# Spreading reciprocal softmax sums over partitions: by TensorE or by small DMAs through DRAM

## What is computed

```python
# second stage: t is (4, 1024, 64)
q, k, v = x @ Wq.T, x @ Wk.T, x @ Wv.T
att = where(causal, q @ k.T / sqrt(64), -inf)
t = t + softmax(att) @ v
# third stage, each step
op = argmax(h[0, 0, :19])
q, k, v = h @ wq[op], h @ wk[op], h @ wv[op]
y = softmax(q @ k.T / sqrt(64)) @ v @ wo[op]
h = where(attn_mask[op], y, h)
z = relu(h @ w1[op] + b1[op]) @ w2[op] + b2[op]
h = where(ffn_mask[op], z, h)
```

## Time and profile before

| | |
|---|---|
| Three timed runs | 822.22, 811.87, 814.77 us; median 814.77 |
| Profiled execution | 811.98 us |
| its span (first to last instruction) | 810.2 us |
| mean granted TensorE clock | 0.975 |
| PE busy | 694.0 us (86%), 3005 instructions |
| DVE busy | 592.1 us (73%) |
| ACT busy | 427.7 us (53%) |
| scan stage | to about 505 us |
| causal attention, groups | about 524 to 608 us |
| feed-forward step alone | about 625 to 648 us |
| expert attention | about 657 to 774 us |
| feed-forward behind it | 777 to 801 us |

### The profile page before, as it was taken

The page is one execution under the profiler, slowest core; times in us unless marked ns, Lnnn a source line. Parts: engine busy times, 40 slices in busy tenths (PEclk is TensorE's granted clock), DMA queues, the critical chain, the costliest instruction groups (busy, mean ns, idle before and its releaser), DMA issues. The chain is left out here.

```text
span 810.2 us, 9559 instructions
## 1 busy us (share of the span) xinstructions
PE 694.0 (86%) x3005; PEld 335.9 (41%) x3005; DVE 592.1 (73%) x624; ACT 427.7 (53%) x656; POOL 457.3 (56%) x234
## 2 busy tenths in 40 slices
PE   4769989889999999998898789789983778999993
PEld 2323333333433333333333333367671225677640
DVE  3489999999899998999998981455552334666633
ACT  2868468477485583784763324545443214555520
POOL 6269999999989999899999994000000000000000
PEclk9999999999999999999999999999997799999997
DMA  3398676675566766656766730000000000000001
GB/s 89 85 274 307 223 235 219 210 262 209 193 229 199 253 227 209 208 214 221 253 208 203 251 116 1 0 1 2 2 2 5 8 17 2 2 2 1 2 1 56
DMA packets 32588, 105.33 MB, mean 130 GB/s; under 512 B 6533, under 2 KB 7182, under 8 KB 32526
## 3 DMA queue, kind: packets, MB, share of 16 engines
q1 hardware_dynamic: 31558, 103.91, 38.3%
q10 hardware_dynamic: 648, 0.55, 0.3%
q0 software_dynamic: 320, 0.13, 0.1%
HBM read 98.80 MB, written 2.10 MB: 125 GB/s over the span
## 5 line engine op out<-in xcount | busy, mean ns | idle before, releaser
L753 POOL TENSOR_TENSOR hc<-hh,cc 128x1024 f32<-128x1024 f32 x128 | 298.9, 2351 | 13.3 <-PE py L257 6.6
L257 PE MATMUL py<-hc,w_cst 128*128 128x512 f32 x512 | 239.7, 596 | 5.7 <-DVE yg L631 4.6
L623 DVE TENSOR_TENSOR_SCAN hh<-da,pb 128x1024 f32<-128x1024 f32 x72 | 164.6, 2286 | 2.5
L257 PEld LDWEIGHTS py<-hc,w_cst 128*128 128x128 f32 x512 | 96.0, 190 | 107.9 <-issue 92.2
L623 DVE TENSOR_TENSOR_SCAN hh<-pb,dbu 128x1024 f32<-128x1024 f32 x56 | 127.5, 2277 | 8.7 <-ACT pb L474 5.2
L764 POOL TENSOR_TENSOR dbu<-bb,dtu 128x1024 f32<-128x1024 f32 x56 | 131.6, 2350 | 0.0
L474 ACT ACTIVATE pb<-dt,w_aneg 128x1024 f32<-128x1024 f32 x56 | 62.5, 1116 | 86.3 <-DVE hh L623 84.5
L618 DVE TENSOR_TENSOR pb<-pb,dtu 128x1024 f32<-128x1024 f32 x72 | 87.6, 1217 | 5.5 <-PE pb L246 3.3
L474 ACT ACTIVATE da<-dt,w_aneg 128x1024 f32<-128x1024 f32 x72 | 81.3, 1140 | 0.4
L246 PE MATMUL pb<-bc,w_sel 128*128 128x512 bf16 x144 | 43.5, 384 | 26.6 <-DVE hh L623 24.5
L1423 POOL MEMSET wa<- 128x128 f32 x4 | 0.6, 212 | 111.8 <-POOLq L1176 111.8
(11 more groups left out here) (289 smaller groups left out, 1037.1 us busy)
## 6 DMA issues: line engine op xcount, KB each, us to landing
cc<-scr SPq DMA_DIRECT2D x128, 512.0 KB, 4.2
bb<-scr SPq DMA_DIRECT2D x56, 512.0 KB, 4.9
w_xs<-hc SPq DMA_DIRECT2D x6, 256.0 KB, 4.6
w_xst<-in_x SPq DMA_DIRECT2D x2, 512.0 KB, 5.2
scr<-bcf SPq DMA_DIRECT2D x8, 128.0 KB, 4.3
w_xs<-dt SPq DMA_DIRECT2D x4, 256.0 KB, 6.2
w_xs<-dtu SPq DMA_DIRECT2D x4, 256.0 KB, 6.3
out<-yy SPq DMA_DIRECT2D x4, 256.0 KB, 3.7
```

The costliest lines, as they stand in the source:

```text
L257: nc.tensor.matmul(py[:, half(h)], ident, hc[u % NHC][:, half(h)], start=(n == 0), stop=(n == NS - 1)).then_inc(hc_used, 1)
L623: nc.vector.tensor_tensor_scan(hh[u % NHH][:, :], decay[:, :], drive[:, :], 0.0, ALU.mult, ALU.add).then_inc(scan_done, 1)
L753: nc.gpsimd.tensor_tensor(hc[u % NHC][:, :], hh[u % NHH][:, :], cc[u % NCC][:, :], ALU.mult).then_inc(hc_done, 1)
```

## The change

The two broadcasts on TensorE and ScalarE's copy are taken out, in both attentions. In their place SyncE, for each group, waits for the reciprocals, writes them (128 by 2 numbers of 4 bytes) from `rc` to a small DRAM tensor `line`, waits until they have landed, and reads each of the two rows back with 64 partitions at once into `rs`. VectorE's output waits for the values and for these reads. `rs`, `rc` and `line` have two places that alternate by group, with waits for both directions. `sp_all` runs all 16 groups in order; in the causal attention it stands behind the mask loads, in the experts behind the loads of `attend` and so ahead of those of `feed`.

```diff
-        self.rb_out = sem("rb_out")
+        self.rc_sent, self.rs_in = [sem(f"rc_sent{i}") for i in range(2)], [sem(f"rs_in{i}") for i in range(2)]
+        self.sp_passed = sem("sp_passed")
+        self.line = nc.dram_tensor(tag + "line", (2, 2, 128), FP32, kind="Internal").ap()
...
+    def prime_sp(self, sp):
+        for i in range(2):
+            sp.sem_inc(self.rc_sent[i], 16 * self.GRP // 2)
+            sp.sem_inc(self.rs_in[i], 32 * self.GRP // 2)
+
+    def sp_settle(self, sp, sem, value):
+
+        if not isinstance(value, int) or value > 0:
+            settle(sp, sem, value, self.sp_passed)
+
+    def sp_inverse(self, sp, k, g):
+
+        i, n = g % 2, self.GRP // 2 * k + g // 2
+        self.sp_settle(sp, self.rc_done, self.GRP * k + g + 1)
+        self.sp_settle(sp, self.rs_in[i], 32 * n)
+        sp.dma_start(self.line[i, :, :].rearrange("r q -> q r"), self.rc[:, 2 * i:2 * i + 2],
+                     allow_slow_non_contiguous=True).then_inc(self.rc_sent[i], 16)
+
+    def sp_spread(self, sp, k, g):
+
+        i, n = g % 2, self.GRP // 2 * k + g // 2
+        self.sp_settle(sp, self.rc_sent[i], 16 * (n + 1))
+        self.sp_settle(sp, self.o_out, self.GRP * k + g - 1)
+        for r in range(2):
+            sp.dma_start(self.rs[C * r:C * r + C, i, :], self.line[i, r:r + 1, :].broadcast_to((C, 128))).then_inc(self.rs_in[i], 16)
+
+    def sp_all(self, sp, k):
+        for g in range(self.GRP):
+            self.sp_inverse(sp, k, g)
+            self.sp_spread(sp, k, g)
...
     def output(self, dve, k, g, to):
 
-        dve.wait_ge(self.rb_out, self.GRP * k + g + 1)
+        dve.wait_ge(self.o_full, self.GRP * k + g + 1)
+        dve.wait_ge(self.rs_in[g % 2], 32 * (self.GRP // 2 * k + g // 2 + 1))
...
-        pe.wait_ge(self.rc_done, self.GRP * k + g + 1)
         atleast(pe, self.o_out, self.GRP * k + g - 1)
-        for r in range(2):
-            i = 2 * (g % 2) + r
-            nc.tensor.matmul(bank[C * r:C * r + C, 128:256], self.rc[:, i:i + 1].broadcast_to((128, C)),
-                             self.w["cst"][:, IDN:IDN + 128], start=True, stop=True)
...
     def dve_inverse(self, dve, k, g):
         dve.wait_ge(self.p_done, 2 * (self.GRP * k + g) + 2)
-        atleast(dve, self.o_full, self.GRP * k + g - 1)
+        atleast(dve, self.rc_sent[g % 2], 16 * (self.GRP // 2 * k + g // 2))
...
-    def act_inverse(self, act, k, g):
...
             sp.dma_start(mask_words[:, 1, :], inp["ffn_mask"].rearrange("(a w) -> a w", a=1)).then_inc(mask_in, 16)
+            at.sp_all(sp, 0)
...
                         sp.dma_start(wa[i][s, s], src).then_inc(att_loaded, 16)
+                at.sp_all(sp, k)
```

More of the change, by code:

```diff
@@ L934, in prime_act @@
     def prime_act(self, act):
-        for sem, count in ((self.q_out, 4), (self.v_act, 2), (self.p_done, 2 * self.GRP), (self.pts_act, 2 * self.GRP), (self.rb_out, self.GRP)):
+        for sem, count in ((self.q_out, 4), (self.v_act, 2), (self.p_done, 2 * self.GRP), (self.pts_act, 2 * self.GRP)):
             act.sem_inc(sem, count)
+    def prime_sp(self, sp):
[21 more added lines that the diff above has]
+            self.sp_spread(sp, k, g)
     def prime_dve(self, dve):
@@ L1165, in act_all @@
                 self.act_project_v(act, k, (3,))
-            if g >= 2:
-                self.act_inverse(act, k, g - 2)
         self.act_turned(act, k, self.GRP - 1)
-        self.act_inverse(act, k, self.GRP - 2)
-        self.act_inverse(act, k, self.GRP - 1)
 def build_attend(nc, w, inp):
@@ L1410, in _ @@
                 sp.sem_inc(loaded, count)
+            at.prime_sp(sp)
             sp.wait_ge(zeroed, 4)
```

## The result

| | before | after |
|---|---|---|
| Timed runs, median | 814.16 us (4 runs) | 964.41 us (4 runs) |
| Profiled execution | 811.98 us | 963.82 us |
| Span | 810.2 us | 962.0 us |
| Mean granted clock | 0.975 | 0.909 |

The ratio is 1.179, with a 95% interval of 1.173 to 1.186: slower by 150 us. The forecast was 810.8 us with a range of 804 to 826.

The account below looks back on a forecast made before the run. The expert attention was taken as bound almost equally by TensorE's work and a loop through ScalarE. Terms -2.0 - 0.4 + 0 + 0.1 - 0.3 = -2.6 us took 813.4 to 810.8 us, range 804 to 826.

Parts of the forecast that it names:

- the write's price: SyncE's write of reciprocals to DRAM, both attentions: 2.4 us from issue to landing, with 1.9 and 6.9 as ends.
- The first rival: Both attentions: slow DRAM write of 4.3 us makes SyncE the bound, backlog and longer tails, +23 to 834 us; chance 0.14.
- long past: VectorE's reciprocal waits for the write of two groups before, which was claimed to be finished long before.
- SyncE free: Expert attention: SyncE is free again after 4.4 us against a period of 5.94, so no stall: 0.
- 5.94 us: Expert attention: group period falls from 6.08 us, scores starting 0.14 earlier; -2.0 us over 14 steady groups.
- the copy on ScalarE gives nothing: Expert attention: the 0.29 us copy stands ahead of an idle stretch of 2.64 us, so removing it saves nothing.
- The price of 0.22 for a group's broadcasts: TensorE, both attentions: most that removing the two broadcasts can give per group, in us; 7.0 over 32 groups.
- stalls begin from w = 3.05: Causal attention: a write this long, in us, uses up group 1's 1.3 us of slack by two writes in a row.
- The forecast's sum: Whole kernel: -2.0 expert loop, -0.4 causal joins, 0 stalls, +0.1 causal tail, -0.3 expert tail; -2.6 us.
- Its causal tail: End of the causal attention: last reciprocal's end to last output goes from 5.36 to 5.45 us; +0.1.
- The move of the weights: Expert tail: feed-forward weights queue behind all sixteen groups; first feed-forward matmul 8.7 us after last reciprocal's end, before 8.98; -0.3.
- covered: Expert tail: last output, at 5.8 + 0.1 us, needed only by the last of four output projection matmuls, so no cost.

Follow-up runs that it names:

- The probes: Kernel before with twelve extra DMAs of various forms on SyncE in the causal attention, waited for by SyncE alone; three probes: 815, 810 and 812 us.
- the turned write: Changed kernel with VectorE transposing the reciprocals first, so the write is two DMAs of 4 pieces of 128 bytes; 813.79 us, ratio 0.9996 to the kernel before.
- the pairs: Changed kernel with each reciprocal written twice side by side, making the write 256 packed pieces of 8 bytes; 821.91 us, ratio 1.010.
- the last version: Kernel before in the causal attention, DMA chain with 8 pieces of 128 bytes in the expert one; 811.00 us, ratio 0.9958 to the kernel before.
- the doubled ones: Kernel before with both broadcasts done twice on TensorE, same values; ratio 1.012, expert period from 6.08 to 6.30 us.

## Why the prediction was wrong

**The step that failed** is the write's price, "scattered numbers cost some 0.4 more: w = 2.4 us". It measured 8.0 in the causal attention and 7.8 in the expert one (7.2 to 9.8), above even the upper end of 6.9 that I had given it. I had taken the size of the write from a DRAM write of 128 KB in long rows and the surcharge for its form from a load of 4-byte numbers. Each row was right; they don't add. The probes show it in one place: 4-byte pieces into SBUF 1.98 us, long rows into DRAM 1.17 to 1.60, 4-byte pieces side by side into DRAM 8.1. The form costs where small pieces are written next to each other in DRAM, and no row of the trace held that.

**The first rival was right in kind.** Its mechanism (SyncE's cycle against the reciprocals' pace, then both tails) is what happened; I gave it 0.14 and priced it at w = 4.3. With the measured 8.0, its own working gives a causal cycle of 9.4, 15 x (9.4 - 4.76) = 70, an expert cycle of 10.0, 15 x (10.0 - 5.94) = 61, and 5.6 for each tail: 810.8 + 142 = 953 us against 964.4. By the table the attentions with their tails hold 145.7 us of loss, 4 more than that, and 6.1 lie outside them. The split differs: 63.0 and 52.8 between the reciprocals, 16.2 and 13.7 in the tails, as the reciprocals run ahead of SyncE (the last causal write was issued at 676.1, 10.7 us behind its reciprocal). Among what the working lacks are the spreads, 3.4 us in place of 2.1, and issues like this one of 2.96 us for one of a pair that took 0.6 elsewhere:

```profile
825.86 2.96 SPq L964
```

Two more steps were off. The prediction held that VectorE's reciprocal would find the write of two groups before "long past"; it waited for it 16 times. And its own terms for the expert attention make SyncE free after 4.1 us, not 4.4 (w + 1.7, not w + 2.0); the measured distance of 10.1 us with a write of 7.8 is nearer to the stated value.

**The range was too narrow by its own rows.** It stopped at w = 3.9, while the row of the same queue's DRAM writes went to 6.9. I set that row aside because the DMA share was 0.01, which answers contention but not form. The sentence of the Trainium skill (DMA: Bandwidth & Descriptors, Anatomy of one DMA, a section on DMAs issued by GpSimd, where these are SyncE's) on long confirmations of writes to HBM pointed to the right side, and the trace now agrees for this form, with 8.0 us, but not for writes to DRAM as such, with 1.17.

**Right were** the steps on the engines. "5.94 us" for the expert loop is what the turned write, the pairs and the last version all show within 0.02 us, once the DMA hides; TensorE's 20.00 of 20 was not the only limit. That the copy on ScalarE gives nothing fits that 5.94, but wasn't tried by itself. The price of 0.22 for a group's broadcasts was met by the doubled ones. That stalls begin from w = 3.05 fits the pairs at 3.3. The forecast's sum, -2.6 us or -0.3%, is within what the turned write measured (-0.04%, +-0.35%), which can't tell it from no change either. Its causal tail, from the start of the last reciprocal to the last output, was 6.1 us in place of the 5.6 of my sum, as the longer reciprocal and the transposition are added to it.

**The move of the weights** did no harm of its own: in the changed kernel they are issued at 917.77, behind all groups, but the last output comes only at 919.99; and in the last version, where the chain is short, the feed-forward starts 9.07 us behind the last reciprocal, against 9.13 before (my sum had 8.7 from the reciprocal's end, which is 8.8 from its start). The timeline of the changed kernel shows what the prediction called "covered" and wasn't:

```profile
919.99 0.29 DVE L980 TENSOR_TENSOR yy<-ex_rb,ex_rs 128x128 f32<-128x128 f32 x1 [8.97 <-DMA ex_rs<-ex_line]
920.20 1.28 DVE L1530 COPY w_h<-ex_pt 128x512 f32<-128x512 f32 x2
921.02 3.75 PE L1456 MATMUL ex_pt<-yy,wa 128*128 128x512 f32 x4 [12.34 <-DVE w_h L1530]
```

The copies of the output projection stand behind the last output in VectorE's list, so not only the last of the four matmuls but the second half of them, and all behind it, waited for that output.

## What to carry to other kernels

Price a DMA by its destination and the length of its pieces together: a row for the destination and another for the piece length don't add up to it. Before small numbers are laid side by side in DRAM from many partitions, turn them into runs (here 8 runs of 128 bytes: 1.2 us in the probe against 8), or keep the few matmuls that do the job on chip. And a queue that waits out each transfer has a pace of its own: compare write + wait + issues with the period of the loop that it serves before calling a transfer hidden.

## What the runs showed of the hardware that I had not expected

- A write of 256 packed pieces of 4 bytes to DRAM is confirmed after 7.4 to 8.4 us in the probes (7.2 to 9.8 in the changed kernel); the same count of packed 8-byte pieces after 2.9 to 3.8, of 16-byte pieces after 1.7, 4-byte pieces 16 bytes apart after 2.3. Sixteen packed pieces alone take 1.75, 64 take 7.05.
- Reads issued on SyncE's queue 0.5 us behind such a write landed after 6.5 us, with the write; with no write under way they took 3.4.
- A reciprocal on VectorE takes 155 ns for 2 numbers a partition, 343 for 32 and 943 for 128, so 6.3 ns for each further number; a copy of 512 numbers out of PSUM takes about 690 ns.
- Two broadcast matmuls of 64 columns take TensorE no longer than one of 128: 5.06 us from the scores to the transposes of r = 0 with either.
